# Between batches, ScalarE rounds VectorE's products to the high parts; steps are written into m_pos and masked in place

## The reference

```
h  = einsum('bnf,hfo->bhno', x, W)          # x (8,2048,512), W (8,512,64)
s1 = einsum('bhno,ho->bhn', h, a1)
s2 = einsum('bhno,ho->bhn', h, a2)
e  = leaky_relu(s1[..., :, None] + s2[..., None, :], 0.2)
attn = softmax(where(adj > 0, e, -9e15), axis=-1)
out  = layernorm(x + concat_heads(einsum('bhnm,bhmo->bhno', attn, h)))
```

## Time and profile before

| what | us |
|---|---|
| median of three runs | 3096.35 |
| the profiled execution | 3097.49 |
| its span, first to last instruction | 3095.8 |
| DVE busy | 2825.2 (91%) |
| PE busy | 2660.4 (86%) |
| ACT busy | 2283.5 (74%) |
| POOL busy | 822.4 (27%) |
| mean granted TensorE clock | 0.966 |

### The profile page before, as it was taken

How to read it: one execution, slowest core, us unless ns; L and a number is a source line. 1 busy time by engine, 2 the same in 40 slices (tenths; PEclk the granted TensorE clock), 3 DMA queues, 4 the chain that set the end, 5 groups by cost and what they waited for, 6 DMA issues and landing times.

```text
span 3095.8 us, 93392 instructions
## 1 busy us (share of the span) xinstructions
PE 2660.4 (86%) x36162; PEld 2283.5 (74%) x36162; DVE 2825.2 (91%) x4249; ACT 2283.5 (74%) x3782; POOL 822.4 (27%) x1011
## 2 busy tenths in 40 slices
PE   4998889888898898988989889888888988888885
PEld 2488865888568885788847888488874888758885
DVE  4899988999889998899988999899997999889997
ACT  2399972999649995599946998279973999739994
POOL 2512115121242113322143221522215121151211
PEclk9999999999999999999999999999999999999998
DMA  5346633575435654266542675336644466345653
GB/s 164 88 105 160 154 99 99 126 161 138 115 81 130 159 135 134 56 153 155 135 111 64 157 163 124 98 82 161 154 113 113 96 159 153 103 105 118 161 141 91
DMA packets 281087, 388.19 MB, mean 125 GB/s; under 512 B 161856, under 2 KB 161856, under 8 KB 280672
## 3 DMA queue, kind: packets, MB, share of 16 engines
q1 hardware_dynamic: 253536, 315.24, 38.5%
q0 software_dynamic: 27136, 67.12, 12.9%
HBM read 313.52 MB, written 34.14 MB: 112 GB/s over the span
## 4 chain that ended last, share of the span: by engine, by line
DVE 63%; issue 17%; PE 11%; ACT 4%; DVEq 1%; POOL 1%; ACTq 0%; POOLq 0%
DVE m_neg L802 16%; DVE m_pos L795 10%; DVE step L780 9%; PE ps L475 8%; DVE neg_part L638 5%; ACT step L573 4%; DVE total L632 4%; DVE neg_part L640 3%; DVE total L642 3%; DVE xmax L624 2%; PE ps L501 2%; DVE y L666 2%; DVE ln_stats L653 1%; DVE prod L768 1%; PE ps L531 1%
## 5 line engine op out<-in xcount | busy, mean ns | idle before, releaser
L573 ACT ACTIVATE step<-ps,s_steep 128x512 fp8e4<-128x512 f32 x3328 | 1959.2, 760 | 604.1 <-PE ps L426 304.9
L501 PE MATMUL ps<-b_both,m_pos 128*128 128x130 f16 x16384 | 1052.2, 225 | 293.8 <-DVE total L632 271.1
L501 PEld LDWEIGHTS ps<-b_both,m_pos 128*128 128x128 fp8e5 x16384 | 998.8, 101 | 327.6 <-issue 326.7
L531 PE MATMUL ps<-d_both,m_neg 128*128 128x130 f16 x16384 | 976.1, 221 | 24.3 <-DVE neg_part L638 24.3
L531 PEld LDWEIGHTS ps<-d_both,m_neg 128*128 128x128 fp8e5 x16384 | 953.6, 98 | 52.3 <-issue 39.9
L795 DVE TENSOR_TENSOR m_pos<-step,maskT 128x1024 uint32<-128x1024 uint32 x512 | 615.7, 1241 | 70.2 <-ACT step L573 36.7
L802 DVE TENSOR_TENSOR m_neg<-m_pos,maskT 128x2048 uint32<-128x2048 uint32 x256 | 584.0, 2281 | 0.4
L475 PE MATMUL ps<-W_sb,xT 128*128 128x512 f32 x1024 | 464.0, 615 | 47.2 <-DVE prod_d L771 46.8
L957 POOL TENSOR_TENSOR den_scaled<-den_inv,bound 128x4 f32<-128x4 f32 x256 | 74.9, 293 | 1524.3 <-DVE den_inv L644 1463.4
L475 PEld LDWEIGHTS ps<-W_sb,xT 128*128 128x128 f32 x1024 | 201.4, 198 | 304.4 <-issue 242.3
L780 DVE TENSOR_SCALAR step<-s_bc,s_neg 128x512 fp8e5<-128x512 f32 x768 | 391.9, 566 | 9.5 <-DVE s_neg L739 3.5
(11 more groups left out here) (90 smaller groups left out, 1536.2 us busy)
## 6 DMA issues: line engine op xcount, KB each, us to landing
adj_in<-in_adj SPq DMA_DIRECT2D x266, 512.0 KB, 4.9
s_bc<-s_rows SPq DMA_DIRECT2D x258, 256.0 KB, 3.7
x_in<-in_x SPq DMA_DIRECT2D x144, 256.0 KB, 4.8
x_sum<-in_x POOLq DMA_DIRECT2D x128, 256.0 KB, 5.8
y<-in_x POOLq DMA_DIRECT2D x32, 1024.0 KB, 9.1
out<-y SPq DMA_DIRECT2D x32, 1024.0 KB, 7.2
maskT<-adj_cut SPq DMA_TRANSPOSE x264, 4.0
W_sb<-in_L_gnn_W SPq DMA_DIRECT2D x4, 256.0 KB, 7.1
```

The source lines that it names most:

```text
L501: mm = pe.matmul(acc, mask, b_both[:, j, h, :, :], start=(j == 0), stop=(j == JC - 1))
L531: mm = pe.matmul(acc, mask, d_both[:, j, h, :, :], start=(j == 0), stop=(j == JC - 1))
L573: ins = nc.scalar.activation(chunk(step[qd], c, 0, BLK), ps[:, BANK_S1 + h % 2, :], ACT.Relu, bias=s2_steep[:, j, h:h + 1], scale=STEEP, s ...
```

## The change

VectorE makes only the two full f32 products of a chunk, into two buffers each (`prods`, `prods_d`). ScalarE copies each to f16, which is the high part (`make_hi`), and GpSimd subtracts as before. TensorE refills a bank on `full_d_made`, VectorE's second product. The cutting of block 0's pieces and the comparison for unit 1 are put between the chunks on ScalarE. VectorE's mask work and layer norm stand behind other chunks than before. In the unit phase the steps are written into `m_pos` itself and masked in place; the writers wait for `neg_made` and `pos_summed` of two units earlier instead of ScalarE waiting for `pos_made` of the unit before.

```
-def cuts_of(k, h):
-    if k == 0:
-        return CUTS_EARLY.get(h, ()), CUTS_LATE.get(h, ())
-    return CUTS[h], ()
...
-        prod = sb("prod", [P, 512], F32)
-        prod_d = sb("prod_d", [P, 512], F32)
+        prods = [sb(f"prod{i}", [P, 512], F32) for i in range(2)]
+        prods_d = [sb(f"prod_d{i}", [P, 512], F32) for i in range(2)]
...                                              # TensorE, projection
                     if jc >= 3:
-                        pe.wait_ge(hi_d_made, b * JC + jc - 2)
+                        pe.wait_ge(full_d_made, b * JC + jc - 2)
...                                              # ScalarE
-            def compare(u, h):
-                act.wait_ge(s1_spread, u + 1)
+            def compare(u, h, first=0, last=len(ACT_CHUNKS)):
+                if first == 0:
+                    act.wait_ge(s1_spread, u + 1)
+                    act.sem_inc(waited[act.engine], 1)
+                    act.wait_ge(neg_made, at(neg_made, u - 1))
+                    act.sem_inc(waited[act.engine], 1)
+                    act.wait_ge(pos_summed, at(pos_summed, u - 1))
+                    act.sem_inc(waited[act.engine], 1)
+                for n in range(first, last):
+                    j = ACT_CHUNKS[n]
+                    ins = nc.scalar.activation(chunk(m_pos[h % 2], j, 0, BLK), ...)
...
+            def make_hi(b, jc):
+                act.wait_ge(full_b_made, b * JC + jc + 1)
+                act.sem_inc(waited[act.engine], 1)
+                nc.scalar.activation(b_hi[:, jc, :, 0:O], prods[jc % 2][:]..., ACT.Copy
+                                     ).then_inc(hi_b_made, 1)
+                act.wait_ge(full_d_made, b * JC + jc + 1)
+                act.sem_inc(waited[act.engine], 1)
+                nc.scalar.activation(d_hi[:, jc, :, 0:O], prods_d[jc % 2][:]..., ACT.Copy
+                                     ).then_inc(hi_d_made, 1)
...
+                for jc in range(JC):
+                    make_hi(b, jc)
+                    if jc < 2:
+                        cut_piece(PIECES * (KB * b + 1) + jc, jc % 2, ...)
+                    elif jc < 8:
+                        compare(b * UNITS + 1, 1, 2 * (jc - 2), 2 * (jc - 1))
+                    elif jc == 8:
+                        compare(b * UNITS + 1, 1, 12)
+                    elif jc < 15:
+                        i = jc - 7
+                        cut_piece(PIECES * (KB * b + 1) + i, i % 2, ...)
...                                              # VectorE, split_chunk
                 dve.wait_ge(h_summed, b * JC + jc + 1)
-                V.tensor_tensor(b_hi[:, jc, :, 0:O], bank, kb, ALU.mult)
-                dve.wait_ge(lo_made, at(lo_made, 2 * JC * b + 2 * jc - 1))
-                V.tensor_tensor(full_b, bank, kb, ALU.mult).then_inc(hi_b_made, 1)
-                V.tensor_tensor(d_hi[:, jc, :, 0:O], bank, kd, ALU.mult)
-                dve.wait_ge(lo_made, at(lo_made, 2 * JC * b + 2 * jc))
-                V.tensor_tensor(full_d, bank, kd, ALU.mult).then_inc(hi_d_made, 1)
+                dve.wait_ge(lo_made, at(lo_made, 2 * JC * b + 2 * jc - 3))
+                V.tensor_tensor(full_b, bank, kb, ALU.mult).then_inc(full_b_made, 1)
+                dve.wait_ge(lo_made, at(lo_made, 2 * JC * b + 2 * jc - 2))
+                V.tensor_tensor(full_d, bank, kd, ALU.mult).then_inc(full_d_made, 1)
...                                              # VectorE, compare(u, h, nth)
+                dve.wait_ge(neg_made, at(neg_made, u - 1))
+                dve.sem_inc(waited[dve.engine], 1)
+                dve.wait_ge(pos_summed, at(pos_summed, u - 1))
+                dve.sem_inc(waited[dve.engine], 1)
                 dve.wait_ge(s1_loaded[hp], 16 * (nth + 1))
                 dve.sem_inc(waited[dve.engine], 1)
...                                              # VectorE, make_pos
-                    dve.wait_ge(pos_summed, at(pos_summed, u - 1))
                     dve.wait_ge(step_dve, at(step_dve, u + 1))
                 dve.wait_ge(step_act, at(step_act, QUADS * u + qd + 1))
-                V.tensor_tensor(words(m_pos[hp][:, js, :]), words(step[qd][:]),
+                V.tensor_tensor(words(m_pos[hp][:, js, :]), words(m_pos[hp][:, js, :]),
                                 words(mask[:, js, :]), ALU.bitwise_and).then_inc(pos_made, 1)
...                                              # VectorE, between the chunks
-                    if jc in (4, 6):
-                        make_pos(b * UNITS + 1, 1, maskT[0], jc // 2 - 2)
-                    if jc == 9:
+                    if jc in (7, 9):
+                        make_pos(b * UNITS + 1, 1, maskT[0], jc // 2 - 3)
+                    if jc == 11:
                         make_neg(b * UNITS + 1, 1, maskT[0])
-                    for when, work in ((11, ln_first_half), (12, ln_statistics), (14, ln_apply)):
+                    for when, work in ((8, ln_first_half), (10, ln_statistics), (13, ln_apply)):
...                                              # GpSimd: buffers prods[jc % 2], prods_d[jc % 2]
-                    if jc == 12:
+                    if jc == 11:
                         with pool.If(b > 0):
                             deviation(KB * b - 1)
```

More of the change, by code:

```diff
@@ L78, in gat_kernel @@
     H_BANKS = (7, 6, 4)
+    ACT_CHUNKS = [j for j in range(JC) if j % JQ not in DVE_SLOTS[j // JQ]]
     PARTS = 3
@@ L125, in gat_kernel @@
         m_neg = [sb(f"m_neg{i}", [P, JC // 2, 2 * BLK], FP8) for i in range(2)]
-        step = [sb(f"step{i}", [P, JQ // 2, 2 * BLK], FP8) for i in range(QUADS)]
         s1_bc = [sb(f"s1_bc{i}", [P, BLK], F32) for i in range(2)]
@@ L218, in gat_kernel @@
         h_summed = sem("h_summed")
+        full_b_made = sem("full_b_made")
+        full_d_made = sem("full_d_made")
         hi_b_made = sem("hi_b_made")
         hi_d_made = sem("hi_d_made")
-        lo_made = sem("lo_made", free=1)
+        lo_made = sem("lo_made", free=3)
         x_added = sem("x_added", free=2)
@@ L238, in gat_kernel @@
         pos_made = sem("pos_made", free=QUADS)
-        neg_made = sem("neg_made", free=0)
+        neg_made = sem("neg_made", free=1)
         pos_read = sem("pos_read", free=0)
@@ L362, in _ @@
                                 load_x(JC * (b + 1) + t, t % 2, ((b + 1) * (JC // 2) + t // 2) % (NBLK * IT // 2))
-                        for i in cuts_of(k, h)[0] + cuts_of(k, h)[1]:
+                        for i in CUTS[h] if k else range(PIECES) if h == 0 else ():
                             sp.wait_ge(neg_made, at(neg_made, H * g))
@@ L562, in exponentials @@
                 nc.scalar.activation(r_next[:], r_in[:], ACT.Exp, scale=SLOPE - 1.0).then_inc(exp_made, 1)
-            def compare(u, h):
-                act.wait_ge(s1_spread, u + 1)
-                act.sem_inc(waited[act.engine], 1)
-                for qd in range(QUADS):
-                    act.wait_ge(pos_made, at(pos_made, QUADS * (u - 1) + qd + 1))
-                    act.sem_inc(waited[act.engine], 1)
-                    for c in range(JQ):
-                        if c not in DVE_SLOTS.get(qd, ()):
-                            j = qd * JQ + c
-                            ins = nc.scalar.activation(chunk(step[qd], c, 0, BLK), ps[:, BANK_S1 + h % 2, :], ACT.Relu,
-                                                       bias=s2_steep[:, j, h:h + 1], scale=STEEP, saturate=False)
-                    ins.then_inc(step_act, 1)
+            def compare(u, h, first=0, last=len(ACT_CHUNKS)):
[8 more added lines that the diff above has]
+                    j = ACT_CHUNKS[n]
+                    ins = nc.scalar.activation(chunk(m_pos[h % 2], j, 0, BLK), ps[:, BANK_S1 + h % 2, :], ACT.Relu,
+                                               bias=s2_steep[:, j, h:h + 1], scale=STEEP, saturate=False)
+                    if n + 1 == len(ACT_CHUNKS) or ACT_CHUNKS[n + 1] // JQ > j // JQ:
+                        ins.then_inc(step_act, 1)
@@ L595, in _ @@
                         u = g * H + h
-                        early, late = cuts_of(k, h)
-                        for i in early:
+                        for i in CUTS[h] if k else ():
                             cut_piece(PIECES * (g + 1) + i, i % 2, (g + 1) * IT + i // 2)
@@ L605, in _ @@
                             copy_s1(b + 1)
-                        if unit < UNITS - 1:
+                        if unit == 0:
+                            pass
+                        elif unit < UNITS - 1:
                             compare(u + 1, (h + 1) % H)
@@ L613, in _ @@
                                 compare(u + 1, 0)
-                        for i in late:
-                            cut_piece(PIECES * (g + 1) + i, i % 2, (g + 1) * IT + i // 2)
         @block.vector
@@ L760, in split_chunk @@
                 bank = ps[:, H_BANKS[jc % 3], :].rearrange("p (h o) -> p h o", h=H)
-                full_b = prod[:].rearrange("p (h o) -> p h o", h=H)
-                full_d = prod_d[:].rearrange("p (h o) -> p h o", h=H)
```

(4 more changed lines are left out.)

15 lines of the change are left out of this document (9 added, 6 removed).

## The result

The changed kernel took 3108.09 us, the median of seven runs (3105.71 to 3114.16), against 3096.88 us of seven runs of the kernel before. The ratio is 1.0035, with a 95% interval of 1.0025 to 1.0045. It is slower by 0.35%; the forecast was 3077, faster by 0.6%. The profiled execution took 3105.71 us, its span is 3104.0.

A forecast was written before the change was run, and what follows sets the result against it. VectorE was taken to bound the unit phase, TensorE the stage between batches. 9.5 + 10.3 + 9 - 1.5 - 7.4 = 19.9 us off 3097.5 gave 3077.6, 3076.5 from the median; forecast 3077, range 3062 to 3096.

The forecast's parts named there:

- The fourth chunk: Stage between batches: TensorE's bank is free after VectorE's second product, two steps earlier; 1.2 us a batch, 9.5 us gained.
- The last chunk and the clock behind it: Stage's end: shorter chain gains 1.5 us in seven batches, 10.3 in all; the clock no longer falling gains 9 us.
- the clock rival: Stage's end: the shorter wait still suffices for the granted clock to fall; 3086 us, chance 0.15.
- The chain of 3.05 us: Last chunk, from TensorE's transposes of x through VectorE's product, ScalarE's copy and GpSimd's subtraction to TensorE: 3.05 us.
- The GpSimd rival: Stage's end: GpSimd, late from moved mask work, does not recover and the last chunk gains nothing; 3087 us, chance 0.06.
- ScalarE's queue: Stage: cuts in their new places make the last cut slightly late; 0.2 us a batch, 1.5 us lost, ends 0 and 44.
- The first rival: Stage: cuts ahead of ScalarE's copies, a pair taking 10.16 us, start unit 0 late; 3119 us, chance 0.08.
- The projection: Stage, from the fourth chunk on: TensorE's 104 instructions without a gap still take about 47 us.
- the clock ahead of it: Wait ahead of the fourth chunk: the clock's fall there counted as no change; 16 us better if it went.
- VectorE's queue: Unit phase: two new always-met waits ahead of comparisons cost 42 ns in 22 a batch; 7.4 us lost, ends 0 and 23.
- The rival for it: Unit phase: each unit pays 0.13 us for VectorE's new waits; 3092 us, no change that can be told, chance 0.09.
- the signs: Profile marks expected: fourth-chunk wait 3.3 us, low-part wait ending at 3.05, comparison 0.17 behind reciprocal; VectorE waiting in units refutes.

The follow-up runs named there:

- the best kernel: Changed kernel without the two wait pairs, `s1_loaded`'s pair moved ahead of the read-out of the negative sums, `ln_apply` behind chunk 15 instead of 13: 3040.13 us, ratio 0.9816.

## Why the prediction was wrong, point by point

**The fourth chunk: right.** Forecast 1.2 us a batch, measured 20.04 - 18.85 = 1.19.

**The last chunk and the clock behind it: right in sum to 0.5 us, one step wrong.** Forecast 1.5 + 1.6 us in a later batch; from the transposes of x to the spread the second batch gained 9.04 - 6.38 = 2.66, and the seven later ones 2.35 on average, where 2.8 were in the sum. The clock's part came in full in the profiled execution; in other kernels with the same tail it came in some batches only, so the clock rival was half true. The chain of 3.05 us is right where nothing disturbs it, 3.08 in the first batch and 3.15 with `ln_apply` last; the copy itself took 0.63 us and not 0.70. I had worked with 2.71 us for `ln_apply`, its time beside a GpSimd that was not behind; at its new place GpSimd was still working off `m_neg` and `deviation`, and it took 4.17. The GpSimd rival, priced at 10 us, came in part.

**ScalarE's queue: right.** Its waits for `adj_in` fell from 131.4 to 47.6 us, 39 times in each, of which six stand in the stages of the seven later batches, the longest 1.6 us. The last cut was late by the products of chunk 14, not by a load. The first rival, the only one that I had ending slower, did not occur.

**The projection: right to 0.7 us.** 104 instructions in 46.6 us where they took 47.17 in the second batch. Over the seven later batches, start to transposes, the mean fell from 47.27 to 46.61, because the time at half clock fell from 5.1 to 3.3 us a batch. That is 5 us over the run which the sum put at nothing ("the clock ahead of it"); its rival case, 16 us, came by a third.

**VectorE's queue: the step that failed.** It was put at "two more are 42 ns", 7.4 us over the run, with 23 us as its end. It cost 5.0 us a batch, 40 us: 0.22 us at each comparison and not 0.042. With its real price the sum is 3077 + 33 = 3110, against 3108 measured; that it comes so near is in part luck, since the projection gave 5 us more and the last chunk with its clock 16 us where 19 were summed. The mechanism and its place behind the reciprocal were as described; the size was off, and a little the count. Of the nine comparisons behind layer norm, which were to hide the pairs, three stand behind the last instruction of `ln_statistics` and pay as well, so it is 24 a batch and not 22. For the size there were two mistakes. The price was taken from the duration row of one instruction, which says how long that row is and not how far apart two instructions of the queue can follow; and of four added instructions I counted the two increments and not the two waits. And the end of 23 us took the 0.13 us of the earlier trace rows for the most that two pairs can cost, where that is the distance with one pair, in which the reciprocal still hides a part: without any pair it is 0.10. Nothing in those rows bounds a second and a third pair. The nearest bound from the other side would have been that one pair per 0.13 us makes 0.26 for two, 46 us, and with that end in the range it would have reached to 3116.

The rival for it was named, and given 0.09, at 3092; that too is 16 us below what was measured. For it spoke what decided the case: VectorE has no slack in the unit phase, so that each 0.1 us ahead of a comparison is paid 192 times.

Of the signs, two said that the forecast was wrong where it was: the comparison stood 0.35 us behind the reciprocal and not 0.17, and VectorE waited in the unit phase, 192 times. Two more were off without costing much: the wait ahead of the fourth chunk, 4.1 to 5.7 us and not 3.3, and TensorE's wait behind the transposes of x, which ended 2.63 us behind them with all four groups of matmuls, 3.75 us, still to come. The forecast had it end at 3.05 us, with 2.9 us to come.

## What to carry to other kernels

On an engine that sets the pace, a wait that is always met is not free: count waits and increments as instructions, look for what runs ahead of them in the same queue, and put them behind a long instruction and never behind a short one. Where a trace shows no idle time and the engine is the bound, the distance between the starts of short instructions is worth reading; here a third of the win of the best kernel, 20 of 56 us, came from there, out of a place that the change had not touched. That all this holds for other short instructions than this reciprocal was not tried. And a wait that an engine repeats for a count it has itself waited for already can go.

## What the runs showed of the hardware that was not expected

A met wait with its increment costs VectorE's stream 0.11 us where only a 0.18 us reciprocal and another such pair stand ahead of it, and nothing that can be seen behind an instruction of 2.28 us; the increment's own row shows a median of 21 ns in both cases.

VectorE's `tensor_scalar` on four 128x512 tiles took 2.71, 3.63 and 4.17 us, with GpSimd's subtractions beside it for 1.5, 2.5 and 3.4 us, and a subtraction beside it took up to 1.33 us instead of 1.12: both lose. It costs only where someone waits for it, as in the second case nobody did.

TensorE's same wait at the same place, 1.8 to 2.0 us, was followed by a fall of the granted clock to 0.50 in none, one and three of seven batches of three kernels that differ only in the two pairs of VectorE's queue (the changed kernel, the one without them, the one with them elsewhere).
